# A cross-attention and expert layer: a packing load issued a round later, an inverse deviation on other engines, and the last scores in other banks

## The reference, cut to what matters

```python
def _L0_xattn_ref(query, key, value, key_padding_mask, ...):      # 16 heads of 16
    q, k, v = split_heads(query, Wq, bq), split_heads(key, Wk, bk), split_heads(value, Wv, bv)
    scores = einsum('bhqd,bhkd->bhqk', q, k) / sqrt(16)
    scores = where(key_padding_mask, -inf, scores)
    attn = softmax(scores) @ v
    return attn.reshape(B, Sq, E) @ Wo.T + bo

def _L0_ffn_ref(x, Wr, W1, W2):                                   # 8 experts, 640 slots each
    probs = softmax(x @ Wr);  idx = argmax(probs);  pmax = max(probs)
    pos = rank of the token among those of its expert;  kept = pos < 640
    expert output = relu(slots @ W1[e]) @ W2[e]
    return where(kept, expert output * pmax, x)

x = x + _L0_xattn_ref(_layernorm(x), ctx, ctx, mask, ...)
x = x + _L0_ffn_ref(_layernorm(x), Wr, W1, W2)
```

## Time and profile before

| | |
|---|---|
| runs | 505.53, 507.38, 508.52 us (median 507.38) |
| profiled execution | 504.69 us, span 503.0 us, mean granted clock 0.98 |
| PE busy | 463.8 us (92%), 3009 instructions |
| DVE, POOL, ACT busy | 208.6, 191.2, 140.7 us |
| chain that ended last, by engine | PE 55%, DMA 24%, SP's queue 12%, issue 3%, POOL 3% |
| DMA | 60.66 MB, mean 121 GB/s |

### The profile page before, as it was taken

How to read it: one execution, slowest core, us unless ns; L and a number is a source line. 1 busy time by engine, 2 the same in 40 slices (tenths; PEclk the granted TensorE clock), 3 DMA queues, 4 the chain that set the end, 5 groups by cost and what they waited for, 6 DMA issues and landing times.

```text
span 503.0 us, 8150 instructions
## 1 busy us (share of the span) xinstructions
PE 463.8 (92%) x3009; PEld 312.4 (62%) x3010; DVE 208.6 (41%) x607; ACT 140.7 (28%) x203; POOL 191.2 (38%) x336
## 2 busy tenths in 40 slices
PE   7999879989999989797947999999999999999995
PEld 3443425334443525142714889989999999899894
DVE  5877436667665646373631331131131131313211
ACT  1135344454535454437201220010010110102000
POOL 5742824465866271827474231101111111131212
PEclk9999999999999999899969999999999999999998
DMA  6998624542434252424115160060240340634000
GB/s 191 308 241 187 220 84 150 149 142 74 155 103 160 88 158 68 156 93 153 53 41 169 55 226 33 18 238 22 66 179 22 115 149 15 236 98 155 19 21 12
DMA packets 49950, 60.66 MB, mean 121 GB/s; under 512 B 4802, under 2 KB 40617, under 8 KB 49904
## 3 DMA queue, kind: packets, MB, share of 16 engines
q1 hardware_dynamic: 42224, 47.49, 31.1%
q0 software_dynamic: 3456, 7.35, 4.3%
q10 hardware_dynamic: 4224, 5.21, 3.4%
HBM read 31.79 MB, written 26.62 MB: 116 GB/s over the span
## 4 chain that ended last, share of the span: by engine, by line
PE 55%; DMA 24%; SPq 12%; issue 3%; POOL 3%; DVE 2%; ACT 1%; POOLq 0%; DVEq 0%; ACTq 0%
DMA strips<-shared 21%; PE tps L1719 11%; PE wk L1729 11%; PE tps L1739 11%; PE wk L1747 10%; SPq L438 6%; SPq L418 3%; SPq L429 3%; PE nat L1296 2%; PE wk L1350 2%; PE nat L1707 1%; PE nat L1417 1%; PE wk L1527 1%; POOL slot_rows L578 1%; PE wk L1475 1%
## 5 line engine op out<-in xcount | busy, mean ns | idle before, releaser
L669 POOL DMA_INDIRECT out_x<-attn_mem,dest x40 | 39.0, 975 | 182.6 <-DVE attn_mem L1261 179.9
L709 ACT ACTIVATE shared<-tps,mask_key 77x1024 f32<-77x1024 f32 x64 | 67.6, 1106 | 27.8 <-PE tps L1442 27.7
L941 DVE TENSOR_REDUCE rowmax<-nat 128x8 f32<-128x616 f32 x58 | 45.9, 791 | 49.2 <-PE nat L1417 49.2
L1729 PE MATMUL wk<-w_sb,shared 128*128 128x256 f32 x256 | 57.7, 379 | 0.0
L1719 PE MATMUL tps<-shared,w_sb 128*128 128x256 f32 x256 | 56.6, 379 | 0.8 <-ACT shared L812 0.8
L1739 PEld LDWEIGHTS tps<-shared,w_sb 128*128 128x128 f32 x480 | 56.0, 192 | 0.8
L1739 PE MATMUL tps<-shared,w_sb 128*128 128x128 f32 x480 | 56.0, 275 | 0.0
L1747 PE MATMUL wk<-w_sb,shared 128*128 128x256 f32 x240 | 54.3, 379 | 0.0
L1719 PEld LDWEIGHTS tps<-shared,w_sb 128*128 128x128 f32 x256 | 48.6, 190 | 7.5 <-issue 1.0
L1729 PEld LDWEIGHTS wk<-w_sb,shared 128*128 128x128 f32 x256 | 48.0, 190 | 6.2
L1417 PE MATMUL nat<-kblk,qT 64*128 64x308 f32 x232 | 46.3, 473 | 4.1 <-DVE rowmax L941 3.8
(11 more groups left out here) (195 smaller groups left out, 556.8 us busy)
## 6 DMA issues: line engine op xcount, KB each, us to landing
w_sb<-in_w SPq DMA_DIRECT2D x12, 1024.0 KB, 8.8
strips<-shared SPq DMA_DIRECT2D x28, 256.0 KB, 3.8
slot_rows<-zeros SPq DMA_DIRECT2D x1, 5340.0 KB, 30.4
x_sb<-slot_rows SPq DMA_DIRECT2D x7, 667.5 KB, 4.4
x_sb<-in_x SPq DMA_DIRECT2D x8, 512.0 KB, 8.8
w_sb<-in_w ACTq DMA_DIRECT2D x4, 1024.0 KB, 7.5
out_x<-base SPq DMA_DIRECT2D x8, 512.0 KB, 3.8
attn_mem<-strips SPq DMA_DIRECT2D x28, 128.0 KB
```

Of the source, the lines that this page charges most:

```text
L669: pool.indirect_dma_start(out_rows, bass.IndirectOffsetOnAxis(ap=dest[n % 2][:, c:c + 1], axis=0), y_sb[n % 2][:, c, :], None, bounds_chec ...
L709: act.activation(probsT[0:SK, r % 2, 2 * i:2 * i + 2, :], tps[0:SK, 2 * i:2 * i + 2, :], ACT.Exp, bias=mask_key[:, g // GPB:g // GPB + 1]) ...
L941: dve.tensor_reduce(rowmax[:, j, :, m, :], nat_heads(g, k), AX.X, ALU.max).then_inc(rowmax_ready, 1)
L1729: last = pe.matmul(wk[(SC * n + c) % 2][:, 0:D], hidden[:, f, c * P:(c + 1) * P], w2_sb[n % 2][:, f, :], start=(f == 0), stop=(f == FC - 1))
```

## The change

Three things are changed.

- SP: `pack_strips(c, k)` is issued one round later, behind the gathering and the store of round k + 1; that of round 3 is issued in the next step, ahead of `spread`.
- The last group's inverse deviation is no longer made by POOL. DVE adds the epsilon, ACT takes the square root and copies the mean (with a first square root on other data before the bias of the last logits), and DVE computes the inverse with one Newton step, behind `place(LAST)`. `dispatch(LAST)` waits for these instead.
- The last group's scores of round 1 go to `nat` and the two work banks, which are now one tensor `work`, and those of round 2 to `tps` at once after them. The values of round 0 go to bank `nat[:, 0]`. The eight filler products of that place are left out, and the order of the last group's work on ACT and PE is adapted.

```diff
@@ -165,7 +165,7 @@
         var1, y1, yy1, rstd1 = (sb(f"ln1_{i}", [P, TPG]) for i in range(4))
-        var2, y2, yy2, rstd2 = (sb(f"ln2_{i}", [P, TPG]) for i in range(4))
+        var2, y2, yy2, rstd2, std2 = (sb(f"ln2_{i}", [P, TPG]) for i in range(5))
@@ -217,7 +217,8 @@
         nat = ctx.enter_context(nc.psum_tensor("nat", [P, 2, 512], F32))
-        wk = [ctx.enter_context(nc.psum_tensor(f"wk{i}", [P, 512], F32)) for i in range(2)]
+        work = ctx.enter_context(nc.psum_tensor("work", [P, 2, 512], F32))
+        wk = [work[:, i, :] for i in range(2)]
@@ -229,6 +230,17 @@
+
+        def scores_banks(g, r, i):
+
+            if (g, r) == (LAST, 1):
+                return work if i else nat
+            return tps[:, 2 * i:2 * i + 2, :]
+
+        def attn_bank(g, r):
+            if g == LAST:
+                return wk[0] if r else nat[:, 0, :]
+            return wk[1 if r == 3 else 0]
@@ -302,6 +314,11 @@
         rstd2_step = sem("rstd2_step")
+        last_var_ready = sem("last_var_ready")
+        last_std_ready = sem("last_std_ready")
+        last_mean_ready = sem("last_mean_ready")
+        last_rstd_step = sem("last_rstd_step")
+        last_rstd_ready = sem("last_rstd_ready")
@@ -457,6 +474,7 @@
                 if has(r):
+                    pack_strips(r, 3)
                     spread(r)
@@ -464,9 +482,11 @@
                         store_strips(c, k)
-                        pack_strips(c, k)
+                        if k > 0:
+                            pack_strips(c, k - 1)
             pipeline(step)
+            pack_strips(LAST - 1, 3)
             spread(LAST - 1)
@@ -572,7 +592,11 @@
-                wait(pool, rstd2_step, 8 * g + 8)
+                if g < LAST:
+                    wait(pool, rstd2_step, 8 * g + 8)
+                else:
+                    pool.wait_ge(last_rstd_ready, 1)
+                    pool.wait_ge(last_mean_ready, 1)
                 wait(pool, route_ready, g + 1)
@@ -648,7 +672,6 @@
             dispatch(LAST - 1)
-            second_rstd(LAST)
             dispatch(LAST)
@@ -706,7 +729,7 @@
                     wait(act, scoresT_ps, 2 * (ROUNDS * g + r) + i + 1)
-                    act.activation(probsT[0:SK, r % 2, 2 * i:2 * i + 2, :], tps[0:SK, 2 * i:2 * i + 2, :], ACT.Exp,
+                    act.activation(probsT[0:SK, r % 2, 2 * i:2 * i + 2, :], scores_banks(g, r, i)[0:SK, :, :], ACT.Exp,
                                    bias=mask_key[:, g // GPB:g // GPB + 1]).then_inc(probsT_ready, 1)
@@ -714,7 +737,7 @@
                 wait(act, sums_loaded, 16 * ROUNDS * g)
-                act.copy(attnU[:, r, :], wk[1 if r == 3 and g < LAST else 0][:, :]).then_inc(attnU_ready, 1)
+                act.copy(attnU[:, r, :], attn_bank(g, r)).then_inc(attnU_ready, 1)
@@ -771,8 +794,9 @@
             exponentials(LAST, 1)
+            wait(act, attn_ps, ROUNDS * LAST + 1)
+            exponentials(LAST, 2)
             copy_attn(LAST, 0)
-            exponentials(LAST, 2)
             copy_attn(LAST, 1)
@@ -780,7 +804,12 @@
             copy_back(1)
+            act.activation(std2[:, 0:1], averager[:, 0:1], ACT.Sqrt).then_inc(last_std_ready, 1)
             bias_logits(LAST)
+            act.wait_ge(last_var_ready, 1)
+            act.wait_ge(last_std_ready, 1)
+            act.activation(std2[:, :], var2[:, :], ACT.Sqrt).then_inc(last_std_ready, 1)
+            act.copy(rows[LAST % 2][:, :, MEAN], mv2[:, :, 0]).then_inc(last_mean_ready, 1)
@@ -1182,8 +1211,19 @@
             second_moments(LAST)
+            dve.wait_ge(moments2, NG)
+            dve.tensor_scalar(var2[:, :], mv2[:, :, 1], EPS, None, ALU.add).then_inc(last_var_ready, 1)
             masked_positions(LAST)
             place(LAST)
+            dve.wait_ge(last_std_ready, 2)
+            dve.reciprocal(y2[:, :], std2[:, :]).then_inc(last_rstd_step, 1)
+            dve.wait_ge(last_rstd_step, 1)
+            dve.tensor_tensor(yy2[:, :], var2[:, :], y2[:, :], ALU.mult).then_inc(last_rstd_step, 1)
+            dve.wait_ge(last_rstd_step, 2)
+            dve.scalar_tensor_tensor(rstd2[:, :], yy2[:, :], -0.5, y2[:, :], ALU.mult, ALU.mult).then_inc(last_rstd_step, 1)
+            dve.wait_ge(last_rstd_step, 3)
+            dve.scalar_tensor_tensor(rows[LAST % 2][:, :, RSTD], rstd2[:, :], 1.5, y2[:, :], ALU.add, ALU.mult
+                                     ).then_inc(last_rstd_ready, 1)
@@ -1433,13 +1473,16 @@
                     wait(pe, picks_ready, 3)
-                wait(pe, probsT_ready, 2 * (ROUNDS * g + r))
+                if g == LAST and r in (1, 2):
+                    wait(pe, probsT_ready, 2 * ROUNDS * g + 2 * (r - 1))
+                else:
+                    wait(pe, probsT_ready, 2 * (ROUNDS * g + r))
                 for q in range(4):
                     of = slice(q * QUARTER, (q + 1) * QUARTER)
-                    pe.matmul(tps[0:SK, q, :], minus_piece[of, r, :], maxT[of, :], start=True, stop=False)
+                    pe.matmul(scores_banks(g, r, q // 2)[0:SK, q % 2, :], minus_piece[of, r, :], maxT[of, :], start=True, stop=False)
                 for q in range(4):
                     of = slice(q * QUARTER, (q + 1) * QUARTER)
-                    last = pe.matmul(tps[0:SK, q, :], kblk[of, b, m, (q % 2) * 2 + par, :], qT[g % 2][of, m, :],
+                    last = pe.matmul(scores_banks(g, r, q // 2)[0:SK, q % 2, :], kblk[of, b, m, (q % 2) * 2 + par, :], qT[g % 2][of, m, :],
                                      start=False, stop=True)
@@ -1449,12 +1492,16 @@
                 if r == 0:
-                    if g > 1:
+                    if g == LAST:
+                        wait(pe, probsT_ready, 2 * (ROUNDS * g + 1) + 1)
+                    elif g > 1:
                         wait(pe, posm_ready, g - 1)
...
                         wait(pe, xnT_ready[1], 2)
+                elif (g, r) == (LAST, 1):
+                    wait(pe, posm_ready, LAST - 1)
                 elif g == LAST or r == 1:
@@ -1469,7 +1516,7 @@
                 wait(pe, probsT_ready, 2 * (ROUNDS * g + r) + 2)
-                bank = wk[1 if r == 3 and g < LAST else 0]
+                bank = attn_bank(g, r)
                 for q in range(4):
@@ -1654,13 +1701,13 @@
             wait(pe, attnU_ready, ROUNDS * LAST)
-            keep_warm(8)
+            wait(pe, posm_ready, LAST - 1)
             scores(LAST, 1)
+            scores(LAST, 2)
             weigh_values(LAST, 0, None, None, LAST - 1, LAST - 2)
-            scores(LAST, 2)
             weigh_values(LAST, 1, None, None, LAST - 1, LAST - 2)
+            scores(LAST, 3)
             transpose_strips(0)
-            scores(LAST, 3)
             transpose_strips(1)
...
             router_of_attn(LAST - 1, None, LAST)
```

## The result

The changed kernel takes 494.24 us (median of four runs, 492.62 to 495.37) against 507.95 us before (505.53 to 509.28, four runs on the same chip): a ratio of 0.973 with a 95% interval of 0.968 to 0.978. The forecast was 496.9 in a range of 491.5 to 502.5. In the profiled executions it is 495.37 against 504.69, spans 493.6 and 503.0.

A forecast was written before the change was run, and what follows sets the result against it. SP's queue, waiting for strip stores to land, was taken to bound the loop. 10.8 - 0.5 - 0.3 + 0.5 = 10.5 us off 504.69 gave 494.2, put at 496.9 for the median, range 491.5 to 502.5.

The forecast's parts named there:

- SP held the loop: Loop: SP's transfers and four rounds of store landings, some 25.3 us, are as long as a step of 26 to 29.
- Size of the loop: Steps 1 to 6: steps 1 to 5 gain 7.7 us, step 6 gains 3.1, sum 10.8, less 0.5 for contention.
- The contention with the weight loads: Steps 1 and 2: expert weights loading slow the stores; 0.5 us taken back, bounds 0 and 3.
- The last group: Group 7's scores and values: gain 0; slower store landing costs 0.3 us, fallen clock 0, up to 2.
- the anchor: Group 6's router product stays 13.94 us behind the last group's first score, set by the broadcasts, with 2.2 us idle.
- The tail: End of dispatch: scatter 3.4 us earlier, but 36 filler products end last, so gain 0.5 us, bounds 0 and 3.4.
- The table load: ScalarE's square root before the last logits' bias: one load of 1.28 us, cost taken as 0, bounds 0 and 1.5.
- The signs: Trace marks named beforehand for right (such as steps near 25.6 us) and wrong (a step above 26.5, clock 0.50).
- Rival 1: Tail pays in full because the filler is no bound: 2.9 us more, 494.0 us; chance 0.14.
- rival 3: Loop step was never SP's; only the clock comes back, some 2 us: 505.4 us; chance 0.05.
- rival 4: Slower: stores paired with loads land in 8.16 us and delay the broadcasts, about 512.5 us; chance 0.05.
- rival 2: Half is eaten by contention in steps 1 and 2 and two clock falls, step 6 and last stage: 503.1 us; 0.16.

The follow-up runs named there:

- pack_only: Kernel before with only the SP part of the change, all packing loads a round later: 495.51 us, ratio 0.979 to the kernel before.
- last_round_only: Kernel before with only the packing load of round 2 moved, behind the gathering and store of round 3: 494.25 us, ratio 0.976.
- pack_rstd: The change without its third part (the last group's scores), so packing loads and inverse deviation only: 491.09 us, ratio 0.972 to the kernel before.
- whole_again: The whole change itself, unaltered, measured once more in another set: 492.79 us, ratio 0.971 to the kernel before.
- rstd_only: Kernel before with only the last inverse deviation taken off GpSimd: 505.42 us, ratio 0.999.
- scores_only: Kernel before with only the last group's scores and values in other banks and order, without the eight filler products: 507.36 us, ratio 0.999.
- spread_pool_26: Whole change with four of group 6's eight broadcasts issued by GpSimd and 26 filler products at the end: 490.12 us, ratio 0.966 to the kernel before.
- pack_rstd_fill26: The change without its third part, with 26 instead of 36 filler products ahead of the first transposes: 489.67 us, ratio 0.967 to the kernel before.
- spread_act: Whole change with four of group 6's eight broadcasts issued by ScalarE instead of SP: 494.73 us, ratio 0.979 to the kernel before.

## Why the prediction was right, point by point

- **SP held the loop.** Right, and shown: `pack_only` has most of the gain, with no wait of ScalarE for the sums left, and `last_round_only` shows that one landing too many was the whole of it. The prediction's list of four landings in a step was true, but once one is out the other three cost nothing.
- **Size of the loop.** Forecast 10.8 less 0.5. Steps 1 to 6 gave 10.5 us in the profiled pair. Steps 2 to 5 went to 25.3 to 25.7 instead of 25.64, step 6 to 25.05 instead of 25.2. That the sum came out to 0.2 us is luck: steps 2 to 6 were 1.0 us better than forecast and step 1 was worse. It took 27.06, 1.4 more than forecast: the clock fell at 59 to 65 us (granted 0.50 at 60 to 62), which also cost the 1.1 us ahead of it. In `pack_rstd`, whose program is the same up to there, it did not fall and group 7 starts at 212.96 instead of 215.76; in `whole_again`, the same kernel, at 212.85, and there steps 1 to 6 gained 12.4 us. The contention with the weight loads, 0.5 with bounds to 3, did not show: step 2 took 25.31.
- **The last group.** Right about the anchor: 13.78 us with 2.27 of idle (forecast 13.94 and 2.2), gain 0.2. The likeliest case took the clock as staying up; it fell, in both traces, for 1.6 and 2.6 us (router product to the values of round 3, 4.56 and 5.57 instead of 2.94). This is the term that was sized wrong, though inside its bound of 2 in the first trace and beyond it in the second. The landing slowed by the load beside it, 0.3 with bounds 0 and 1, did not show: the store landed in 2.12 us instead of 3.01. What did slow was the landing of the broadcasts, which the prediction took as unchanged: 0.8 us in the first trace after, 1.8 in the second, so that the product stood 13.78 and 14.80 us behind the first score. In the first this just made up for the 0.9 us by which the broadcasts left earlier; that the anchor held to 0.2 us is in part luck.
- **The tail.** Right that the filler takes over from the scatter and cuts 3.4 us down; the size was 0.5 forecast against 1.8 in the profiled pair (1.1 in `rstd_only`). This is the other term that was sized wrong, the end of the filler, put 1.1 us later than before. Measured from the totals (255.33 and 247.64) it ended 14.3 us behind them before and 14.4 after. Its start was 0.5 us later (first weight load 3.5 us behind the totals before, at 258.80, and 4.0 after; the row at 259.20 counts only 35 of the 36 products), and it ran 0.5 us shorter. Its length is no constant, 10.9 us in `rstd_only`, 10.5 after and 9.5 in `whole_again`, by how long it ran at the lower clock. So the gain is no constant either: from totals to the first expert product `whole_again` has 14.82 us, 0.9 less than the first trace after.
- **The table load.** 0 was right: the bias behind it ended 0.7 us before TensorE turned to the logits (last section).
- **From 504.69 to the median.** The forecast moved the profiled pair's difference onto the median. The kernel before varied from 501.8 to 510.4 us over its runs, and its profiled execution was a fast one in that spread; the one after was the slowest of its four. What part of the 13.7 us each fall of the clock makes can't be read from times alone. That part stays open. The forecast lay 2.7 us from the median although four of its terms were each off by a microsecond or more (step 1, the stretch ahead of group 1, the clock in the last group, the tail); they pull both ways, and that the total is so close is in part luck.
- **The signs.** Most of the signs of being right came true. Two signs of being wrong showed all the same: a step above 26.5 us (step 1) and granted clock 0.50 inside the loop (60 to 64 us) and behind the router product (230 to 232 us). They marked falls of the clock, not a fault in the account of SP's queue. And the filler's start, expected over 1 us later against the last group, was 0.8 later (first weight load 5.76 us behind the last group's count at 253.04 before, 6.52 behind the one at 245.12 after).

Rival 1 (the whole 3.4 us, because the filler is no bound) is refuted in its first half: the transposes still stand directly behind the filler. Its reason, a slow part of the filler that shrinks, came true in part and is worth more than the 0.14 it was given: 1.8 us gained in the first trace after and 2.7 in `whole_again`, where the granted clock was back at 1.00 from 256 us on (after, from 258). The median of 494.24 lies at that rival's 494.0. Refuted are also rival 3 by `pack_only` and `last_round_only`, rival 4 by steps of 25.3 us. Of rival 2's two falls of the clock one happened, ahead of the projection; the contention it added did not show.

## What to carry to other kernels

When a queue issues a small transfer that others wait for, add up the landings that the queue sits through ahead of it, and compare the sum with the step: taking one landing out of the list gave 12.1 us in its set, taking out all four gave 10.2 in its own, and the two ratios (0.976 and 0.979) can't be told apart. That one was enough fits the rows before: the last gathering left 2.3 us too late (3.06 instead of 0.75 into the step), which is less than a landing of 3.7 us. Ask of every stop that is removed what else ends within the same microseconds, filler products included: before the change they ended 1.8 us ahead of what the stage waited for, and after it they were the end. Work that is brought forward in front of a wait that stays only makes the idle longer, and here every idle of over 2 us at that place cost a fall of the clock on top.

## What the runs showed of the hardware

- Idle and clock: behind idles of 2.27, 3.30 and 5.30 us ahead of group 6's router product the granted clock fell to 0.50 (after, `whole_again`, `scores_only`); behind 1.26 and 1.54 us at the same place it stayed (`pack_only`, `spread_pool_26`). Ahead of the first transposes it fell behind 2.49, 2.98 and 4.15 us and stayed behind 1.56 and 1.77. Behind 1.58 us in step 6 it fell in three traces of ten, and at 56 to 60 us it fell in three (after, `pack_only`, `pack_rstd_fill26`) whose longest idle from 44 us on was 0.99 us. Two executions of one program can so be 2.9 us apart at the last group (215.76 and 212.85).
- The square root's table cost 1.28 us and nothing visible beside it: the load starts 0.02 us after the copy ahead of it ends (238.80 + 0.59) and the next activation starts 0.01 us behind the load. By the 2.66 us that the Trainium skill ("ScalarE: Activation LUTs", What ACT_TABLE_LOAD costs) gives for a switch, the bias of the last logits would have ended 1.4 us later and TensorE, which turned to them at 241.85, would have waited 0.7 us. The measurement decides. ACT's timeline after:

```profile
238.80 0.59 ACT L744 COPY attn_mem<-nat 128x512 f32<-128x512 f32 x1 [2.98 <-PE nat L1542]
...
239.41 1.28 ACT L807 ACT_TABLE_LOAD   x1
...
240.70 0.20 ACT L807 ACTIVATE ln<-averager 128x1 f32<-128x1 f32 x1
240.81 0.35 ACT L755 ACTIVATE lgT<-tps,lg_bias 128x128 f32<-128x128 f32 x1
```

- Four of the broadcasts took 2.50 us to issue on GpSimd beside SP. When ScalarE and SP issued four each at once, it was 3.74 and 3.44 us (`spread_act`), against 5.21 for eight on SP alone (after). Beside GpSimd, SP took 2.86 for its four.
